# Quantiser extremes of seven matrices taken in the first projections instead of in the opening

## The chip, the cores and the metric

One core of one Trainium2 chip. The time is that of the whole program on the device in microseconds, the median of several runs. Beside it stands one execution recorded by the hardware profiler; all durations of single instructions come from it.

## What is computed

Two transformer blocks on x, 4096 rows of 256 (4 batches of 1024). The first one, L0, has 16 heads of 16 and quantises each weight matrix as a whole to 8 bits before use; the second, L1, has 16 heads of 64 and plain weights.

```python
def fake_quant_w(w, n_bits=NBITS):
    levels = 2 ** n_bits - 1
    mn = jnp.min(w)
    mx = jnp.max(w)
    delta = (mx - mn) / levels
    zp = jnp.round(-mn / delta)
    wq = jnp.clip(jnp.round(w / delta) + zp, 0, levels)
    wdq = (wq - zp) * delta
    return w + jax.lax.stop_gradient(wdq - w)
...
x = cross_attn(layernorm(x, ln1_g, ln1_b), layernorm(x, ln1_g, ln1_b), q1_w, k1_w, v1_w, o1_w, o1_b) + x
x = cross_attn(layernorm(x, ln2_g, ln2_b), context, q2_w, k2_w, v2_w, o2_w, o2_b) + x
x = geglu_ff(layernorm(x, ln3_g, ln3_b), ff1_w, ff1_b, ff2_w, ff2_b) + x
```

So ten matrices of L0 need a minimum and a maximum over all their elements, and a division, before any of their elements can be quantised: `q1_w`, `k1_w`, `v1_w` and the seven that the kernel calls LATE: `o1_w`, `k2_w`, `v2_w`, `q2_w`, `o2_w`, `ff1_w`, `ff2_w`.

## The kernel before

The program is a row of phases. Each opens its buffers and semaphores, gives every engine one written-out list of instructions, and ends with all engines done and its semaphores cleared. Every engine (SP is a queue of DMA issues) goes through its list in order; a `wait_ge` holds all that stands behind it on that engine.

1. `quantise`. SP loads all ten matrices, then x. VectorE (DVE) takes maximum and negated minimum of each (L288, L289), PE transposes the column of extremes and spreads the result over the partitions (L274, L276), DVE works out five scalars per matrix (`self.scalars`: delta, its reciprocal, zero point, two halves of -delta), then quantises the three matrices that are needed at once in ten turns, and SP stores them.
2. `norm_project` of L0. Eight tiles of 512 rows. In a tile: layer norm (DVE statistics, GpSimd `norm_rstd`, DVE `norm_xhat`, PE transposes, ACT scale), a split of the rows into a high and a low part (ACT `high_rows`, DVE `low_rows`), and four chunks c = 0 to 3 of q and k and four units of v on PE, each as six matmuls of high and low parts. DVE and ACT evict them, SP stores them. The norm of tile t + 2 and `low_rows(t + 1)` (L747, at c == 3) are put between the evictions of tile t. PE waits at the start of each tile for `hi_done` and `lo_done`.
3. `attend_narrow`, the self attention of L0. 16 steps i of 16 slots s. In a slot DVE takes four row maxima of scores for a later step (`top`, L1369), PE makes scores (L1501) and shifted scores (L1518), ACT exponentiates them (L1481), PE multiplies with the values (L1530). Four banks hold what DVE reads, three what ACT reads. The same lists hold the once-only work. DVE: `negate`, `turned`, `normalise`, `low`, `project`. SP: `load(i + 2)`, then `maxima(i + 1)`, and at i == 0 the load of the quantised `o1_w` into `wraw` (L1339), once it is stored. GpSimd: memsets, the addition of the bias to x, then `late_quantise`, which quantises the seven late matrices in 11 pieces of at most 1024 columns (five of 512 columns, six of 1024), 14 instructions each, with the loads and stores issued by GpSimd itself (L396, L428). Ahead of piece 4 it splits `wraw` (`low_weights`, L1350).
4. Cross attention and feed forward of L0, then the same phases of L1 with their own weights.

ACT splits `wraw` too; where it does so is this (L1466 to L1469):

```python
for i in range(STEPS + 1):
    if i == 1:
        act.wait_ge(w_in, 16)
        a_.activation(w_hi[:, :, :], wraw[:, :, :], ACT.Copy).then_inc(w_high, 1)
    for s in range(SLOTS if i < STEPS else 10):
```

`w_hi` is first needed in `project` of step 3, within step 4.

Of the kernel before, what the change touches and what calls it, by code (L numbers as in the profile page):

```python
# [96 lines left out]
class Program:  # L97
# [113 lines left out]
    def quantise(self, x_sb, ident):  # L211
# [4 lines left out]
        for name, rows in mats:  # L216
# [3 lines left out]
            self.wq[name] = nc.dram_tensor("quantised_" + name, (i, o), F32, kind="Internal").ap()  # L220
        K = len(mats)
        now = range(K - len(self.LATE))
        size = where[K - len(self.LATE)][0]
        with ExitStack() as st:
            sb, ps, sem = self.open(st)
            w, t, rest = sb("w", [P, at]), sb("t", [P, size]), sb("rest", [P, size])
# [4 lines left out]
            delta, rdelta, zp, ndh, ndl = (self.scalars[:, k, :] for k in range(5))  # L231
# [4 lines left out]
            w_in = [sem("w_in_" + name) for name, _ in mats]  # L236
            ext_t, ends_b = sem("ext_t"), sem("ends_b")
# [126 lines left out]

    LATE_SIZE = 1024

    def late_buffers(self, sb, sem):
# [6 lines left out]
    def late_quantise(self, pool, s, at_piece, between):  # L374
        g = self.nc.gpsimd
        pieces = []
        for m, name in enumerate(self.LATE):
            i, o = self.i["L0_xattn_" + name].shape
            p = 96 if name in ("k2_w", "v2_w") else P
            rows = min(i, max(1, self.LATE_SIZE // o) * p)  # L380
            for a in range(0, i, rows):
                for b in range(0, o, self.LATE_SIZE):
                    cols = slice(b, min(b + self.LATE_SIZE, o))
                    pieces.append((m, *(x[a:a + rows, cols].rearrange("(c p) n -> p c n", p=p)
                                        for x in (self.i["L0_xattn_" + name], self.wq[name]))))

        shapes = [(src.shape[0], src.shape[1] * src.shape[2]) for _, src, _ in pieces]

# [3 lines left out]
        def load(n):  # L392
            m, src, _ = pieces[n]
            if n >= 2:
                pool.wait_ge(s["out"][n % 2], 16 * (n // 2))
# [33 lines left out]
        for k in range(2):  # L429
            pool.wait_ge(s["out"][k], 16 * ((len(pieces) + 1 - k) // 2))  # L430

# [217 lines left out]

    def norm_project(self, L, x_sb, ident, g, b, wq, wk, wv):  # L650
        nc = self.nc
        planes = (self.q, self.k)
        per = L.dim // P
# [20 lines left out]
        with ExitStack() as st:  # L674
# [11 lines left out]
            c_out = [sem(f"c_out{k}") for k in range(ring)]  # L686
            v_out = [sem(f"v_out{k}") for k in range(2)]
            block = st.enter_context(nc.Block())
# [52 lines left out]
            def _(dve):  # L741
                v = nc.vector

                def low_rows(t):
# [9 lines left out]
                self.norm_xhat(dve, n, x_sb, 1)  # L754
                for t in range(TILES):
# [467 lines left out]
    def attend_narrow(self, L, x_sb, ident, wo, bo):  # L1223
# [43 lines left out]
        with ExitStack() as st:  # L1267
# [32 lines left out]
            def _(sp):  # L1300
# [29 lines left out]
                for i in range(STEPS):  # L1330
# [28 lines left out]
            def _(dve):  # L1359
# [2016 lines left out]
    def build(self):  # L3376
        nc, i = self.nc, self.i
        with ExitStack() as st:
# [3 lines left out]
            self.kept = [st.enter_context(nc.semaphore(f"pool_stored{k}")) for k in range(2 * 3 * 2)]  # L3382
            self.scalars = st.enter_context(nc.sbuf_tensor("quantise_scalars", [P, 5, 10], F32))
            self.late_sems = [st.enter_context(nc.semaphore(f"late_{x}{k}")) for x in ("in", "out") for k in range(2)]
            self.quantise(x_sb, ident)

            def p(name):
                return i["L0_xattn_" + name]
# [5 lines left out]
            L, L1 = Layer("L0", 16, 4, None), Layer("L1", 64, 2, None)  # L3394
            self.norm_project(L, x_sb, ident, p("ln1_g"), p("ln1_b"), q["q1_w"], q["k1_w"], q["v1_w"])
            self.attend_narrow(L, x_sb, ident, q["o1_w"], p("o1_b"))
# [32 lines left out]
```

## Time and profile before

| | |
|---|---|
| median of 3 runs | 4222.43 us (4221.16 to 4227.47) |
| profiled execution | 4226.14 us, span 4224.3 us |
| granted TensorE clock, mean over the span | 0.948 |
| busy share of the span | PE 93%, DVE 65%, ACT 44%, POOL 44% |

How to read it: PE is the matmul engine, DVE VectorE, ACT ScalarE, POOL GpSimd, SP the queue that issues most transfers. A line such as L1369 is one of the kernel file. Times of a timeline count from the start of the span. `[0.53 <-ACT f_h_hi L778]` says that the engine was idle for 0.53 us ahead of the instruction and what released it. The granted clock (PEclk) is a share of 2.4 GHz, so 0.50 is 1.2 GHz. A busy PE is not a PE at its peak.

### The profile page before, as it was taken

How to read it: one execution, taken by the hardware profiler on the slowest of the kernel's cores; microseconds unless marked ns; L12 is line 12 of the kernel's file. 1: busy time of each engine (PE TensorE's matmuls, PEld its weight loads, DVE VectorE, ACT ScalarE, POOL GpSimd, SP SyncE). 2: the span in 40 equal slices, each digit the busy share in tenths (PEclk: the TensorE clock that was granted, in tenths of full speed). 3: DMA queues.
4: the chain of work that ended last, by engine and by line, in shares of the span. 5: the costliest groups of instructions: out<-in, count | busy, mean ns of one | idle time of the engine just before them, and what ended most of it. 6: DMA issues, size and time to landing. Idle time of an engine off the chain costs nothing. (4 is left out here: it accounts for less than half of the span.)

```text
span 4224.3 us, 64439 instructions
## 1 busy us (share of the span) xinstructions
PE 3916.2 (93%) x24639; PEld 2597.8 (61%) x24639; DVE 2766.8 (65%) x4547; ACT 1839.8 (44%) x2746; POOL 1859.1 (44%) x1203
## 2 busy tenths in 40 slices
PE   3799999995898997998999999999999979999899
PEld 2543443433456886885666666666666647777787
DVE  6599999953446654435767666676767637665665
ACT  1367777771453333442333333333333324444333
POOL 1288970001113102004777877877787753222200
PEclk9789999986779998997999999999999989999999
DMA  4734434405631105883211121111112010000100
GB/s 158 181 56 75 60 57 46 45 1 79 106 54 49 25 13 177 305 308 123 73 54 51 51 76 51 51 57 70 51 51 73 29 31 10 10 10 1 42 14 17
DMA packets 314325, 294.96 MB, mean 70 GB/s; under 512 B 133324, under 2 KB 237196, under 8 KB 313764
## 3 DMA queue, kind: packets, MB, share of 16 engines
q1 hardware_dynamic: 311364, 281.88, 25.8%
q0 software_dynamic: 2656, 8.97, 0.7%
q8 instruction: 197, 3.23, 0.3%
q14 instruction: 108, 0.88, 0.1%
HBM read 161.92 MB, written 127.28 MB: 68 GB/s over the span
## 5 line engine op out<-in xcount | busy, mean ns | idle before, releaser
L1741 POOL TENSOR_TENSOR f_sums<-f_sums,f_probs 128x1024 f32<-128x1024 f32 x384 | 915.5, 2384 | 154.6 <-ACT f_probs L1860 116.9
L1860 ACT ACTIVATE f_probs<-f_st 128x1024 f32<-128x1024 f32 x512 | 525.0, 1027 | 938.6 <-PE f_st L1906 933.9
L1758 DVE TENSOR_REDUCE f_mx<-f_s 128x1 f32<-128x512 f32 x1024 | 659.8, 686 | 381.0 <-PE f_s L1883 369.6
L1369 DVE TENSOR_REDUCE f_mx<-f_s 128x1 f32<-128x512 f32 x1024 | 638.7, 683 | 53.2 <-PE f_s L1501 31.2
L1481 ACT ACTIVATE f_probs<-f_st 128x512 f32<-128x512 f32 x1024 | 536.1, 600 | 234.1 <-PE f_st L1518 233.8
L1883 PE MATMUL f_s<-f_k,f_q 64*128 64x512 f32 x3072 | 514.7, 414 | 19.1 <-DMA f_k<-k 12.9
L1906 PE MATMUL f_st<-f_q,f_k 64*128 64x512 f32 x3072 | 486.0, 390 | 1.1 <-ACT f_probs L1860 1.0
L1920 PE MATMUL f_acc<-f_probs,f_v 128*64 128x512 f32 x2048 | 466.1, 597 | 0.0
L1883 PEld LDWEIGHTS f_s<-f_k,f_q 64*128 64x128 f32 x3072 | 341.4, 189 | 166.8 <-issue 112.5
L1906 PEld LDWEIGHTS f_st<-f_q,f_k 64*128 64x128 f32 x3072 | 367.0, 185 | 25.8 <-ACT f_probs L1860 3.8
L1518 PE MATMUL f_st<-f_q,f_k 50*128 50x512 f32 x1024 | 336.1, 480 | 6.6 <-ACT f_probs L1481 6.4
L588 POOL TENSOR_TENSOR f_ve<-f_var,f_const 128x4 f32<-128x4 f32 x48 | 10.0, 209 | 698.4 <-DVE f_var L569 698.2
L1518 PEld LDWEIGHTS f_st<-f_q,f_k 50*128 50x128 f32 x1024 | 137.5, 188 | 283.7 <-ACT f_probs L1481 262.6
L1920 PEld LDWEIGHTS f_acc<-f_probs,f_v 128*64 128x64 f32 x2048 | 141.5, 137 | 266.1 <-issue 257.2
L1501 PE MATMUL f_s<-f_k,f_q 48*128 48x512 f32 x1024 | 267.9, 457 | 22.8 <-DMA f_k<-k 22.5
L1530 PE MATMUL f_acc<-f_probs,f_v 128*32 128x512 f32 x2048 | 279.3, 619 | 0.0
L1781 DVE RECIPROCAL f_rd<-f_s 128x512 f32<-128x512 f32 x64 | 214.9, 3358 | 71.7 <-PE f_s L1929 71.7
L1906 PE MATMUL f_st<-f_m,f_mones 64*128 64x512 f32 x1024 | 248.4, 390 | 0.0
L3281 ACT ACTIVATE f_gate<-f_pg,f_bias 128x512 f32<-128x512 f32 x128 | 88.0, 688 | 348.8 <-PE f_pg L3327 348.8
L765 DVE TENSOR_TENSOR f_stage<-f_pc,f_stage 128x512 f32<-128x512 f32 x160 | 110.3, 691 | 190.2 <-ACT f_stage L795 190.1
L1737 POOL TENSOR_TENSOR f_sums<-f_probs 128x1024 f32<-128x1024 f32 x64 | 153.2, 2394 | 184.0 <-ACT f_probs L1860 184.0
L3206 DVE SCALAR_TENSOR_TENSOR f_u<-f_pa,f_bias,f_gate 128x512 f32<-128x512 f32 x128 | 96.1, 751 | 201.4 <-PE f_pa L3327 195.7
(320 smaller groups left out, 7861.8 us busy)
## 6 DMA issues: line engine op xcount, KB each, us to landing
q<-f_stage SPq DMA_DIRECT2D x80, 512.0 KB, 2.9
k<-f_stage SPq DMA_DIRECT2D x80, 512.0 KB, 2.8
f_q<-q SPq DMA_DIRECT2D x32, 1024.0 KB, 5.1
f_k<-k SPq DMA_DIRECT2D x32, 1024.0 KB, 7.5
v<-f_v_stage SPq DMA_DIRECT2D x64, 256.0 KB, 3.1
f_v<-v SPq DMA_DIRECT2D x32, 512.0 KB, 8.7
f_q<-q SPq DMA_DIRECT2D x96, 128.0 KB, 4.3
f_k<-k SPq DMA_DIRECT2D x96, 128.0 KB, 7.1
```

The source lines that it names most:

```text
L1369: v.tensor_reduce(mx[:, i % 2, c:c + 1], bank[u % 4][:, :], AX_X, ALU.max).then_inc(s_free, 1)
L1481: a_.activation(probs[:, n % NP, e % 2, :], stb[k % 3][:, :], ACT.Exp, scale=L.scale).then_inc(p_ready, 1)
L1501: t.matmul(bank[u % 4][:, :], q[cur][rows, j, qb * P:(qb + 1) * P], k_[cur][rows, j, f * HALF:(f + 1) * HALF], start=True, stop=True, tile ...
L1518: t.matmul(stb[n % 3][:, :], k_[cur][rows, j, c * P:(c + 1) * P], q[cur][rows, j, half * HALF:(half + 1) * HALF], start=True, stop=True, t ...
L1530: ins = t.matmul(acc[W * h:W * h + W, :], vs[cur][:, c, h, :], p, start=c == 0, stop=c == KC - 1, tile_position=(0, W * h))
L1741: g_.tensor_tensor(out, out, probs[:, n % NP, :, :], ALU.add).then_inc(sum_done, 1)
L1758: v.tensor_reduce(mx[:, i % 2, c:c + 1], bank[u % 3][:, :], AX_X, ALU.max).then_inc(s_free, 1)
L1781: v.reciprocal(rd[:, half, :], bank[u % 3][:, :]).then_inc(s_free, 1)
L1860: a_.activation(probs[:, s % NP, :, :], stb[s % 2][:, :, :], ACT.Exp, scale=L.scale).then_inc(p_ready, 1)
L1883: ins = t.matmul(bank[u % 3][:, :], q[cur][rows, a, qb * P:(qb + 1) * P], k_[cur][rows, c, f * HALF:(f + 1) * HALF], start=r == 0, stop=r ...
L1906: ins = t.matmul(stb[s % 2][:, h, :], lhs, rhs, start=r == 0, stop=r == 3, tile_position=(64 * h, 0))
L1920: ins = t.matmul(acc[W * h:W * h + W, :], vs[cur][:, c, h, :], probs[:, s % NP, h, :], start=c == 0, stop=c == KC - 1, tile_position=(0, W ...
```

## The change

The opening loads and reduces three matrices in place of ten, and its scalar chain works on three columns in place of ten. The extremes of the seven others are taken piece by piece (the same 11 pieces) in `norm_project` of L0: SP loads the pieces behind the weights, DVE reduces one at c == 1 and one at c == 3 of each tile from tile 2 on. Their 128 x 2 x 11 row extremes are written to DRAM by GpSimd in `attend_narrow` and read back to all partitions; DVE reduces them at i == 0, s == 12 (`late_ends`); GpSimd works out the scalars from them in 40 chained instructions (`late_scalars`) and then quantises the pieces as before. The load of `wraw` waits for 32 in place of 16 on the semaphore that now also counts the write of the row extremes.

```diff
-                for j, (name, rows) in enumerate(mats):
+                for j, (name, rows) in enumerate(mats[0:K]):
                     sp.dma_start(chunks(w, j), dram_view(ins["L0_xattn_" + name], j)).then_inc(w_in[j], 16)
...
+    def late_ends(self, dve, s):
+        v = self.nc.vector
+        dve.wait_ge(s["out"][1], 16)
+        counts = [sum(1 for p in self.late_pieces() if p[0] == m) for m in range(len(self.LATE))]
+        singles = counts.count(1)
+        assert counts[:singles] == [1] * singles
+        for x, op, out in ((0, ALU.max, s["span"]), (1, ALU.min, s["low"])):
+            v.tensor_reduce(out[:, 0:singles], s["rows"][:, x, 0:singles, :], AX_X, op).then_inc(s["top"], 1)
+            at = singles
+            for m in range(singles, len(counts)):
+                v.tensor_reduce(out[:, m:m + 1], s["rows"][:, x, at:at + counts[m], :].rearrange("p k n -> p (k n)"), AX_X, op)\
+                    .then_inc(s["top"], 1)
+                at += counts[m]
+
+    def late_scalars(self, pool, s, c):
...
+        g.dma_start(self.late_rows.rearrange("(x k p) -> p x k", p=P, x=2), self.late_ext[:, :, :], allow_slow_non_contiguous=True)\
+            .then_inc(s["out"][0], 16)
+        pool.wait_ge(s["out"][0], 16)
+        g.dma_start(s["rows"][:, :, :, :].rearrange("p x k m -> p (x k m)"), self.late_rows.partition_broadcast(P))\
+            .then_inc(s["out"][1], 16)
+        c.done(g.memset(levels, float(LEVELS)))
+        c.done(g.memset(rlevels, 1.0 / LEVELS))
+        chained(g.memset(minus, -1.0))
+        pool.wait_ge(s["out"][1], 16)
+        pool.wait_ge(s["top"], 2 * 3)
+        chained(g.tensor_tensor(low, low, minus, ALU.mult))
+        chained(g.tensor_tensor(span, span, low, ALU.add))
...
+        chained(g.tensor_tensor(rdelta, delta, minus, ALU.pow))
...
+        chained(g.tensor_scalar(zp, left, MAGIC, -MAGIC, ALU.add, ALU.add))
...
+        c = Count(pool, s["step"])
         load(0)
-        c = Count(pool, s["step"])
+        self.late_scalars(pool, s, c)
         for k, (m, src, dst) in enumerate(pieces):
...
+                for k, (_, src, _) in enumerate(late):
+                    sp.dma_start(late_w[k][0:src.shape[0], :].rearrange("p (c n) -> p c n", c=src.shape[1]), src).then_inc(late_in[k], 16)
                 for t in range(TILES):
...
+                def extreme(k):
+                    src = late[k][1]
+                    piece_k = late_w[k][0:src.shape[0], :]
+                    dve.wait_ge(late_in[k], 16)
+                    dve.wait_ge(late_done, 2)
+                    for x, op in ((0, ALU.max), (1, ALU.min)):
+                        v.tensor_reduce(self.late_ext[0:src.shape[0], x, k:k + 1], piece_k, AX_X, op).then_inc(late_done, 1)
...
                 for t in range(TILES):
                     for c in range(chunks):
+                        k = ((t - LATE_TILE) * chunks + c) // 2
+                        if c % 2 == 1 and 0 <= k < len(late):
+                            extreme(k)
                         if c == 0 and t + 2 < TILES:
...
                     if i == 0:
-                        sp.wait_ge(late["out"][0], 16)
+                        sp.wait_ge(late["out"][0], 32)
                         sp.dma_start(wraw[:, :, :], wo.rearrange("(c p) d -> p c d", p=P)).then_inc(w_in, 16)
...
                             if f == 0 and s == 10 and i < STEPS:
                                 normalise(2 * i)
+                            if f == 0 and s == 12 and i == 0:
+                                self.late_ends(dve, late)
```

## Rows read from the trace of the kernel before

**Rows 1.** The page, costliest groups: busy us, mean ns; idle before, releaser.

```profile
L1369 DVE TENSOR_REDUCE f_mx<-f_s 128x1 f32<-128x512 f32 x1024 | 638.7, 683 | 53.2 <-PE f_s L1501 31.2
```

**Rows 2.** Timeline of the opening: start us, busy us, engine, line, operation.

```profile
8.27 0.69 DVE L288 TENSOR_REDUCE f_ext<-f_w 128x1 f32<-128x512 f32 x1
...
24.95 2.28 DVE L288 TENSOR_REDUCE f_ext<-f_w 128x1 f32<-128x2048 f32 x1
...
29.57 0.37 PE L274 MATMUL f_pt<-ident,f_ext 128*20 128x128 f32 x1 [29.57 <-DVE f_ext L289]
```

**Rows 3.** Timeline of DVE in one tile of the first projections.

```profile
105.17 0.69 DVE L765 TENSOR_TENSOR f_stage<-f_pc,f_stage 128x512 f32<-128x512 f32 x1 [2.06 <-ACT f_stage L795]
...
107.49 0.69 DVE L765 TENSOR_TENSOR f_stage<-f_pc,f_stage 128x512 f32<-128x512 f32 x1 [0.34 <-ACT f_stage L795]
108.71 1.22 DVE L747 TENSOR_TENSOR f_h_lo<-f_ht,f_h_hi 128x1024 fp32r<-128x1024 f32 x1 [0.53 <-ACT f_h_hi L778]
```

**Rows 4.** Timeline of PE at the edge between two tiles.

```profile
109.14 0.28 PE L827 MATMUL f_pv<-f_w_hi,f_h_lo 128*128 128x256 f32 x1
110.04 0.47 PE L817 MATMUL f_pc<-f_h_hi,f_w_hi 128*128 128x512 f32 x1 [0.62 <-issue]
```

**Rows 5.** Windows: stretch, length, PE, PEld, DVE, ACT, POOL busy, PEclk, DMA, GB/s.

```profile
0.00:56.00 56.00, 0.98 (x3) 0.59 (x3) 44.17 (x81) 0.00 (x0) 0.70 (x6) 1.00 0.56 180
56.00:78.00 22.00, 6.72 (x23) 5.17 (x24) 10.89 (x38) 6.05 (x8) 8.81 (x20) 0.97 0.13 36
```

**Rows 6.** Timeline of GpSimd, small chained instructions of the layer norm.

```profile
59.00 1.02 POOL L590 TENSOR_TENSOR f_rstd<-f_ve,f_const 128x4 f32<-128x4 f32 x1
60.10 0.20 POOL L592 TENSOR_TENSOR f_tmp<-f_rstd 128x4 f32<-128x4 f32 x1
60.38 0.20 POOL L594 TENSOR_TENSOR f_tmp<-f_tmp,f_ve 128x4 f32<-128x4 f32 x1
```

**Rows 7.** Timeline of GpSimd, and one row of DVE, in the self attention.

```profile
220.56 0.95 POOL L396 DMA_DIRECT2D f_late_w<-L_xattn_o_w  x1
...
223.90 0.69 POOL L414 TENSOR_SCALAR f_late_t<-f_late_w,quantise_scalars 128x512 f32<-128x512 f32 x1 [1.69 <-DMA f_late_w<-L_xattn_o_w]
...
246.09 0.82 POOL L428 DMA_DIRECT2D quantised_o_w<-f_late_w  x1 [0.30 <-POOL f_late_w L427]
249.01 0.65 POOL L396 DMA_DIRECT2D f_late_w<-L_xattn_v_w  x1 [2.10 <-DMA quantised_o_w<-f_late_w]
...
329.31 1.29 POOL L1350 TENSOR_TENSOR f_w_lo<-f_wraw,f_w_hi 128x512 fp32r<-128x512 f32 x1
...
429.09 0.69 DVE L1415 TENSOR_TENSOR x_rows<-x_rows,f_s 128x512 f32<-128x512 f32 x1 [0.40 <-PE f_s L1560]
```

**Rows 8.** DMA issues of the whole run: count, KB each, median us to landing.

```profile
f_v<-v SPq DMA_DIRECT2D x128, 32.0 KB, 6.1
...
f_late_w<-L_xattn_ff_w POOLq DMA_DIRECT2D x6, 512.0 KB, 4.1
```

**Rows 9.** Timeline of the self attention around the end of step 0.

```profile
264.50 2.48 DVE L1369 TENSOR_REDUCE f_mx<-f_s 128x1 f32<-128x512 f32 x4
...
271.48 0.58 SPq L1339 DMA_DIRECT2D f_wraw<-quantised_o_w  x1
...
274.61 0.65 ACT L1469 ACTIVATE f_w_hi<-f_wraw 128x512 fp32r<-128x512 f32 x1
```

**Rows 10.** Windows of the granted clock, columns as in rows 5.

```profile
162.00:228.00 66.00, 43.99 (x79) 20.99 (x80) 44.71 (x77) 0.00 (x0) 31.40 (x16) 0.50 0.64 75
...
242.00:246.00 4.00, 4.00 (x23) 2.02 (x23) 2.81 (x5) 2.73 (x6) 3.63 (x3) 0.78 0.01 4
```

**Rows 11.** Timeline of the slots of step 0, PE and ACT.

```profile
235.82 1.93 PE L1530 MATMUL f_acc<-f_probs,f_v 128*32 128x512 f32 x8
...
239.88 1.93 PE L1530 MATMUL f_acc<-f_probs,f_v 128*32 128x512 f32 x8
...
272.68 2.06 ACT L1481 ACTIVATE f_probs<-f_st 128x512 f32<-128x512 f32 x4 [0.54 <-PE f_st L1518]
```

More of the change, by code:

```diff
@@ L220, in quantise @@
             self.wq[name] = nc.dram_tensor("quantised_" + name, (i, o), F32, kind="Internal").ap()
-        K = len(mats)
-        now = range(K - len(self.LATE))
-        size = where[K - len(self.LATE)][0]
+        K = len(mats) - len(self.LATE)
+        now = range(K)
+        size = where[K][0]
+        self.late_rows = nc.dram_tensor("late_extremes", (2 * self.LATE_PIECES * P,), F32, kind="Internal").ap()
         with ExitStack() as st:
             sb, ps, sem = self.open(st)
-            w, t, rest = sb("w", [P, at]), sb("t", [P, size]), sb("rest", [P, size])
+            w, t, rest = sb("w", [P, size]), sb("t", [P, size]), sb("rest", [P, size])
             ext = sb("ext", [P, 2 * K])
@@ L230, in quantise @@
             ends = sb("ends", [P, 2 * K])
-            delta, rdelta, zp, ndh, ndl = (self.scalars[:, k, :] for k in range(5))
+            delta, rdelta, zp, ndh, ndl = (self.scalars[:, k, 0:K] for k in range(5))
             span, levels, rlevels = sb("span", [P, K]), sb("levels", [P, K]), sb("rlevels", [P, K])
@@ L235, in quantise @@
             x_in, id_done, v_done, stored = sem("x_in"), sem("id"), sem("v"), sem("st")
-            w_in = [sem("w_in_" + name) for name, _ in mats]
+            w_in = [sem("w_in_" + name) for name, _ in mats[0:K]]
             ext_t, ends_b = sem("ext_t"), sem("ends_b")
@@ L365 @@
     LATE_SIZE = 1024
+    LATE_PIECES = 11
     def late_buffers(self, sb, sem):
@@ L371, in late_buffers, with late_pieces @@
         s["step"] = sem("late_step")
-        return s
-    def late_quantise(self, pool, s, at_piece, between):
-        g = self.nc.gpsimd
+        n, m = self.LATE_PIECES, len(self.LATE)
+        s["rows"], s["top"] = sb("late_rows", [P, 2, n, P]), sem("late_top")
+        for k in ("span", "low", "levels", "rlevels", "minus", "high_q", "low_q", "left", "part"):
+            s[k] = sb("late_" + k, [P, m])
+        return s
+    def late_pieces(self):
         pieces = []
@@ L385, in late_quantise @@
                                         for x in (self.i["L0_xattn_" + name], self.wq[name]))))
+        assert len(pieces) == self.LATE_PIECES
+        return pieces
+    def late_ends(self, dve, s):
[11 more added lines that the diff above has]
+                at += counts[m]
@@ new lines, in late_scalars, with chained, split, less @@
+    def late_scalars(self, pool, s, c):
+        g = self.nc.gpsimd
+        K = len(self.LATE)
+        first = self.scalars.shape[2] - K
+        delta, rdelta, zp, ndh, ndl = (self.scalars[:, k, first:] for k in range(5))
+        span, low, levels, rlevels, minus, h, l, left, part = (s[k][:, :] for k in (
+            "span", "low", "levels", "rlevels", "minus", "high_q", "low_q", "left", "part"))
+        def chained(ins):
+            c.done(ins)
+            c.wait()
+        g.dma_start(self.late_rows.rearrange("(x k p) -> p x k", p=P, x=2), self.late_ext[:, :, :], allow_slow_non_contiguous=True)\
[10 more added lines that the diff above has]
+        chained(g.tensor_tensor(span, span, low, ALU.add))
+        def split(num):
+            chained(g.tensor_scalar(ndh, num, float(4097), None, ALU.mult))
+            chained(g.tensor_tensor(left, ndh, num, ALU.subtract))
+            chained(g.tensor_tensor(ndh, left, ndh, ALU.subtract))
+            chained(g.tensor_tensor(ndl, num, ndh, ALU.add))
+            chained(g.tensor_tensor(ndl, ndl, minus, ALU.mult))
+        def less(q, d):
+            chained(g.tensor_tensor(part, q, d, ALU.mult))
+            chained(g.tensor_tensor(left, left, part, ALU.add))
+        split(levels)
+        chained(g.tensor_tensor(delta, span, rlevels, ALU.mult))
+        chained(g.tensor_scalar(h, delta, float(4097), None, ALU.mult))
+        chained(g.tensor_tensor(l, h, delta, ALU.subtract))
+        chained(g.tensor_tensor(h, h, l, ALU.subtract))
+        chained(g.tensor_tensor(l, delta, h, ALU.subtract))
+        chained(g.tensor_tensor(part, h, ndh, ALU.mult))
+        chained(g.tensor_tensor(left, span, part, ALU.add))
+        less(l, ndh)
+        less(h, ndl)
+        less(l, ndl)
+        chained(g.tensor_tensor(left, left, rlevels, ALU.mult))
+        chained(g.tensor_tensor(delta, delta, left, ALU.add))
+        chained(g.tensor_tensor(rdelta, delta, minus, ALU.pow))
+        chained(g.tensor_tensor(part, rdelta, delta, ALU.mult))
+        chained(g.tensor_scalar(part, part, -1.0, 2.0, ALU.mult, ALU.add))
+        chained(g.tensor_tensor(rdelta, rdelta, part, ALU.mult))
+        split(delta)
+        chained(g.tensor_tensor(h, low, rdelta, ALU.mult))
+        chained(g.tensor_scalar(h, h, MAGIC, -MAGIC, ALU.add, ALU.add))
+        chained(g.tensor_tensor(left, h, ndh, ALU.mult))
+        chained(g.tensor_tensor(left, left, low, ALU.add))
+        less(h, ndl)
+        chained(g.tensor_tensor(left, left, rdelta, ALU.mult))
+        chained(g.tensor_tensor(left, left, h, ALU.add))
+        chained(g.tensor_scalar(zp, left, MAGIC, -MAGIC, ALU.add, ALU.add))
@@ L387, in late_quantise @@
+    def late_quantise(self, pool, s, at_piece, between):
+        g = self.nc.gpsimd
+        pieces = self.late_pieces()
         shapes = [(src.shape[0], src.shape[1] * src.shape[2]) for _, src, _ in pieces]
@@ L394, in load @@
             if n >= 2:
-                pool.wait_ge(s["out"][n % 2], 16 * (n // 2))
+                pool.wait_ge(s["out"][n % 2], 16 * (n // 2 + 1))
             g.dma_start(part(s["w"][n % 2], n).rearrange("p (c n) -> p c n", c=src.shape[1]), src).then_inc(s["in"][n % 2], 16)
+        c = Count(pool, s["step"])
         load(0)
-        c = Count(pool, s["step"])
+        self.late_scalars(pool, s, c)
         for k, (m, src, dst) in enumerate(pieces):
@@ L429, in late_quantise @@
         for k in range(2):
-            pool.wait_ge(s["out"][k], 16 * ((len(pieces) + 1 - k) // 2))
+            pool.wait_ge(s["out"][k], 16 * ((len(pieces) + 1 - k) // 2 + 1))
     def context_kv(self, L, wk, wv):
@@ L647, with norm_project @@
     H_PASSES = [(k, a, b) for k in range(DC) for a, b in ((0, 0), (0, 1), (1, 0))]
-    def norm_project(self, L, x_sb, ident, g, b, wq, wk, wv):
+    def norm_project(self, L, x_sb, ident, g, b, wq, wk, wv, extremes=False):
         nc = self.nc
+        late = self.late_pieces() if extremes else []
+        LATE_TILE = 2
         planes = (self.q, self.k)
@@ L687, in norm_project @@
             v_out = [sem(f"v_out{k}") for k in range(2)]
+            if extremes:
+                late_w = [sb(f"late_w{k}", [P, src.shape[1] * src.shape[2]]) for k, (_, src, _) in enumerate(late)]
+                late_in, late_done = [sem(f"late_in{k}") for k in range(len(late))], sem("late_done")
             block = st.enter_context(nc.Block())
@@ L754, in _ @@
                 self.norm_xhat(dve, n, x_sb, 1)
+                if extremes:
+                    v.memset(self.late_ext[:, 0, :], -3.0e38).then_inc(late_done, 1)
+                    v.memset(self.late_ext[:, 1, :], 3.0e38).then_inc(late_done, 1)
                 for t in range(TILES):
                     for c in range(chunks):
+                        k = ((t - LATE_TILE) * chunks + c) // 2
+                        if c % 2 == 1 and 0 <= k < len(late):
+                            extreme(k)
                         if c == 0 and t + 2 < TILES:
@@ L3383, in build @@
             self.scalars = st.enter_context(nc.sbuf_tensor("quantise_scalars", [P, 5, 10], F32))
+            self.late_ext = st.enter_context(nc.sbuf_tensor("late_ext", [P, 2, self.LATE_PIECES], F32))
             self.late_sems = [st.enter_context(nc.semaphore(f"late_{x}{k}")) for x in ("in", "out") for k in range(2)]
@@ L3394, in build @@
             L, L1 = Layer("L0", 16, 4, None), Layer("L1", 64, 2, None)
-            self.norm_project(L, x_sb, ident, p("ln1_g"), p("ln1_b"), q["q1_w"], q["k1_w"], q["v1_w"])
+            self.norm_project(L, x_sb, ident, p("ln1_g"), p("ln1_b"), q["q1_w"], q["k1_w"], q["v1_w"], extremes=True)
             self.attend_narrow(L, x_sb, ident, q["o1_w"], p("o1_b"))
```

## The prediction, written before the change was run

> **What bounds the kernel now.** I read the page first, then the timeline of the opening, of one tile of the first projections and of the first two steps of the self attention, with the windows for the granted clock and DMA. The opening is one chain on DVE: the reductions of ten matrices, then a scalar chain and the ten turns of three matrices. PE makes no step before the last extreme: its transpose waits until 29.57, while the first late reduction starts at 8.27 [rows 2]. In the projections PE sets the pace, but each tile starts with a wait: the last matmul of a tile is issued at 109.14, the next tile's first at 110.04 [rows 4], just after `low_rows` ends at 108.71 + 1.23 = 109.94 [rows 3]. In the self attention DVE's 1024 maxima (638.7 us busy, 53.2 us idle in all) set the pace [rows 1], one slot of four per 2.6 us, and ACT has only some 0.5 us of room per slot [rows 11]. PE, DVE and ACT each go through a written-out order, tied by a few PSUM banks: a wait of some ten us on one is a wait of all three.
>
> **The opening.** The fourteen late reductions go: 29.57 - 8.27 is 21.3 us, less 0.1 for the end of the reduction before, so **-21.2 us**. The scalar chain that follows has as many instructions as before, 10 columns or 3 wide, and costs the same. The load of x still lands in time: before it stood behind 4.3 MB more. The seven late loads move to the projections, as 11 issues on SP behind three weight loads.
>
> **Their transfer** runs in a stretch where DMA is busy 0.13, in before's time 60 to 78. 4.3 MB at the 180 GB/s of the opening's average take 24 us, up to 84 [rows 5]. The first tile's stores begin only as this stretch ends, and SP has nothing else to issue before them, so its 11 issues hold up nobody. I take 0 and keep +4 for the range, for what of the transfer reaches past 78. If this cover went, the first tile's stores would be late, then ACT's stage, then PE.
>
> **DVE in the projections.** A 512-wide reduction takes 0.69 us, four in a row 2.48, so 0.60 each [rows 2, 9]; 2048 wide take 2.28 [rows 2], so 1.04 ns per column, and 1024 wide 1.13 us in a row. A pair (maximum and minimum) costs 1.2 us for pieces 0 to 4 and 2.27 for 5 to 10. Pieces with even number stand at c = 1, in an idle 2.06 us [rows 3]: nothing, or 0.2. Odd ones stand before `low_rows`, where idle time is only 0.53 [rows 3], and this is the instruction that PE waits for at the tile's edge [rows 4]. Pieces 1 and 3 cost 0.67 each, 5, 7 and 9 cost 1.74 each: **+6.6 us**. Bounds: 0 if PE's own work hid it, +12 if the whole 20 us of DVE work less its idle time at c = 1 came through.
>
> **The self attention.** This part decides. Before, GpSimd quantises `o1_w` from 223.90, its store is issued at 246.09 and has landed by 249.01 [rows 7]; SP loads it after its maxima at 271.48, and ACT splits it at 274.61 with no idle time before it [rows 9]. That ACT instruction stands at i == 1 ahead of all exponentials of step 1, behind `act.wait_ge(w_in, 16)`, and the change leaves it there. Now the piece can't start before its scalars, and these wait for `late_ends`, which DVE does at i == 0, s == 12. In before's time:
> - Two of the four maxima that start at 264.50 are done at 265.7; `late_ends` starts there [rows 9]. It reads 640, 512 and 256 columns, twice each: 2 x (0.73 + 0.60 + 0.34) = 3.3 us, done at 269.0.
> - GpSimd then issues 40 chained instructions. A small chained one takes 0.28 from start to start (60.10 to 60.38), a power 1.10 (59.00 to 60.10) [rows 6]; 39 x 0.28 + 1.1 = 12.0. The row's power is 4 wide and this one 7, so I take 12.5: 281.5. Bounds 12 to 18: no small tensor_scalar of GpSimd is in the trace.
> - The issue of load(1), 0.7; then piece 0 to landing, 249.01 - 223.90 = 25.1 [rows 7]: 307.3.
> - SP's issue to ACT's split, 274.61 - 271.48 = 3.1 [rows 9]: 310.4.
>
> ACT stood there at 274.61, so step 1 starts **35.8 us** later. What queues behind it: ACT's exponentials; PE's `shifted`, after three banks; PE's scores behind that; DVE's maxima behind those; SP's load(3), which waits for `pv_done`. The 3.3 us of `late_ends` are within the 35.8 and not added. PE runs ahead by under a slot and gets nothing back, since its own time per slot is nearly full.
>
> **The clock.** In the first 66 us around the start of the self attention PE was idle for 22; the granted clock fell to 0.50 (1.2 GHz) and was back only in 242 to 246, at 0.78 on average [rows 10]. At the low level a slot takes 239.88 - 235.82 = 4.06 us, at 2.4 GHz 2.06 + 0.54 = 2.60 [rows 11], so 1.46 us a slot. With its values matmuls PE came back some 7 us after 235.82: two slots, **+3 us**. Bounds 0 and the rival below.
>
> **Of no cost.** The sum moves GpSimd's pieces by 58 us: the split of `wraw` at 329.31 goes to about 388, its first use stands just before 429.09 [rows 7], itself 36 later. The two transfers of the row extremes start at about 221.5, behind load(0) [rows 7], and DVE asks for them at 265.7, 44 us later. The first writes 2816 single elements. 512 short runs land in 6.1 us [rows 8]; one after the other 2816 take 34 us, overlapped far less. The second fills 128 partitions with 1.4 MB; 512 KB land in 4.1 [rows 8], so 11.5. 34 + 11.5 + 2 for the issues is 47, 3 us late at the worst; I take about 20 and no wait. By the Trainium skill (DMA: Bandwidth & Descriptors, Anatomy of one DMA) a transfer from GpSimd costs about 2 us plus bytes over 436 GB/s, which would make the second 5.3 us, an estimate that the 4.1 us for 512 KB agrees with only roughly (3.2 by the rule). Its Rules for kernel authors say that a strided last dimension becomes one descriptor per element, which speaks against the first; no row here shows a store of single elements.
>
> **Sum:** -21.2 + 6.6 + 35.8 + 3 = **+24.2 us**. The profiled execution took 4226.14 us (span 4224.3), 3.7 above the median of the runs, 4222.43; against the first it gives 4250.3, against the median, which is what is timed, 4246.6: **4247 us**.
>
> **Rivals.** What a measurement of this kernel can tell from no change is about 0.2%, 8.4 us.
> - *The stall, as summed* (0.76): 4234 to 4260 (the projections at 0 or 12, the clock at 0 or 8, the chain at 12 or 18, not all at once).
> - *The clock stays low long* (0.05). From 182 to 242 PE was at work and the clock stayed at 0.50: 44 us of busy time before 228 [rows 10], some 58 in all. If it took as long again, 58 / 4.06 = 14 slots x 1.46 = 21 us in place of 3: 4265. Against it: in 182 to 228 PE did nearly only scores of 48 rows. The Trainium skill (TensorE: Matmul & The Clock Gate, What's actually happening) says that the low clock is the default and that activity releases it; by that rule the trace agrees that idling costs, and 4265 hangs on how much PE's mix counts.
> - *DVE waits for the row extremes* (0.07). Its place is `late_ends`; it decides from a landing later than 265.7 on, one for one. With both transfers at 60 us in all it adds 16: 4263.
> - *The other side: ACT isn't held* (0.05). What speaks for it: before, ACT had no idle time at its split [rows 9]. The opening's gain then stands against 6.6 and the 3.3 of `late_ends`: -11.3, 4211. It needs `late_ends` done by 233 instead of 269, against DVE's order; so it would take an order of instructions other than I read.
> - *The two sides nearly cancel* (0.07): the stall at under 30 us, with free extremes and no clock cost. GpSimd would do its 37.6 us of chain and piece in 30 while DVE stands still: 4222.43 - 21.2 + 29 = 4230.
>
> Faster 0.05, same 0.07, slower 0.88. The range reaches from 4232 to 4263: it takes in the first case nearly whole and the wait of DVE, and leaves out the low clock's end, the cancelling and the faster case, 17 in 100 together, and a little of the first case's edges.
>
> **What the profile after would show.** The transpose on PE at about 8.4; `norm_project` starting at about 35; a gap at each tile's edge from tile 2 on, 0.7 then 1.7 us longer. In step 0 of the self attention six reductions at s == 12 without idle time before them; GpSimd's 40 small instructions in about 12.5 us; then an idle time of ACT before its split of some 32 to 36 us, released by the load of `wraw`, with PE and DVE idle as long, and some slots at 1.2 GHz after it. The prediction is wrong if ACT has no such idle time, if GpSimd's chain is far from 12 us, or if DVE sits ahead of `late_ends` waiting for the broadcast.

## The result, and the profile after

The changed kernel takes 4249.75 us (median of 3 runs, 4248.9 to 4258.63) against 4222.43: ratio 1.0073, 95% interval 1.0058 to 1.0089, so it is slower. The ratio isn't the quotient of the two medians: they differ by 27.3 us, the ratio stands for 30.8. The profiled execution of it took 4258.63 us (span 4256.8, mean granted clock 0.945); it was the longest of its three, and is 32.5 us over the profiled one of before. The comparison by place below uses starts of the same instruction in both traces.

The opening, on PE and DVE (timeline; columns as in [rows 2]). The transpose starts at 7.97, in [rows 2] at 29.57:

```profile
7.15 0.68 DVE L290 TENSOR_REDUCE f_ext<-f_w 128x1 f32<-128x512 f32 x1
7.97 0.37 PE L275 MATMUL f_pt<-ident,f_ext 128*6 128x128 f32 x1 [7.97 <-DVE f_ext L290]
```

One tile edge of the first projections, DVE and then PE (timeline). It answers to [rows 3, 4]:

```profile
107.41 0.69 DVE L874 TENSOR_TENSOR f_stage<-f_pc,f_stage 128x512 f32<-128x512 f32 x1 [0.34 <-ACT f_stage L904]
108.01 2.34 DVE L851 TENSOR_REDUCE late_ext<-f_late_w 128x1 f32<-128x1024 f32 x2
110.27 1.22 DVE L842 TENSOR_TENSOR f_h_lo<-f_ht,f_h_hi 128x1024 fp32r<-128x1024 f32 x1
...
111.58 0.47 PE L926 MATMUL f_pc<-f_h_hi,f_w_hi 128*128 128x512 f32 x1 [2.25 <-issue]
...
114.33 1.91 PE L706 MATMUL f_tp<-ident,f_xhat 128*128 128x128 f32 x8
```

`low_rows` (L842) now starts right behind the pair (L851), with no idle time, and PE's gap at the edge is 2.25 us instead of 0.62. The windows that follow show what the gap costs besides itself (columns as in [rows 5]; the clock is the third value from the end):

```profile
110.00:112.00 2.00, 0.41 (x2) 0.40 (x3) 2.00 (x4) 0.00 (x0) 0.00 (x0) 1.00 0.52 145
112.00:114.00 2.00, 2.00 (x11) 1.78 (x10) 1.93 (x10) 0.60 (x1) 0.00 (x0) 0.77 0.51 182
114.00:116.00 2.00, 2.00 (x12) 2.00 (x11) 1.97 (x5) 0.38 (x1) 1.48 (x4) 0.50 0.66 199
```

The clock falls from 1.00 to 0.50 some 1.5 us after PE resumed (0.77 is its mean over 112 to 114). `low_rows` starts at 77.03, 87.76, 98.48, 110.27, 123.64 and 135.43: 0.57, 0.56, 1.63, 3.21 and 1.63 more than the 10.16 us of before, and the last tile loses 1.5 too. The 3.21 holds 1.58 of the low clock.

GpSimd and then DVE at the start of the self attention (timelines); the forecast has nothing that answers to it:

```profile
204.62 1.41 POOL L420 DMA_DIRECT2D late_extremes<-late_ext  x1
220.96 0.57 POOL L423 DMA_DIRECT2D f_late_rows<-late_extremes  x1 [14.94 <-DMA late_extremes<-late_ext]
```

```profile
208.02 7.26 DVE L1478 TENSOR_REDUCE f_mx<-f_s 128x1 f32<-128x512 f32 x12
222.71 3.68 DVE L1478 TENSOR_REDUCE f_mx<-f_s 128x1 f32<-128x512 f32 x6 [7.43 <-PE f_s L1612]
```

DMA issues in the same stretch, 200 to 225 (count, KB each, median us to landing):

```profile
f_late_rows<-late_extremes POOLq DMA_DIRECT2D x1, 1408.0 KB, 11.1
...
f_q<-f_mm SPq DMA_DIRECT2D x4, 8.0 KB, 11.3
late_extremes<-late_ext POOLq DMA_DIRECT2D x1, 11.0 KB, 16.1
```

and of before, in its stretch 214 to 240:

```profile
f_q<-f_mm SPq DMA_DIRECT2D x4, 8.0 KB, 1.9
```

The store of the row extremes took 16.1 us to land. The transfers that put the row maxima into `f_q`, issued after it, landed in 11.3 us instead of 1.9, and PE's next scores, and so DVE, waited 7.4 us for them. The first row maximum of the phase is 14.4 us earlier than before (168.19 against 182.60), the first exponential only 6.0 (222.28 against 228.25).

The end of step 0, all engines (timeline), to be set beside [rows 7, 9]:

```profile
257.13 0.81 DVE L401 TENSOR_REDUCE f_late_span<-f_late_rows 128x5 f32<-128x640 f32 x1
257.86 1.00 DVE L404 TENSOR_REDUCE f_late_span<-f_late_rows 128x1 f32<-128x512 f32 x2
...
260.69 0.20 POOL L430 TENSOR_TENSOR f_late_low<-f_late_low,f_late_minus 128x7 f32<-128x7 f32 x1 [38.97 <-DVE f_late_low L404]
260.97 0.20 POOL L431 TENSOR_TENSOR f_late_span<-f_late_span,f_late_low 128x7 f32<-128x7 f32 x1
...
267.01 1.52 POOL L457 TENSOR_TENSOR quantise_scalars<-quantise_scalars,f_late_minus 128x7 f32<-128x7 f32 x1
...
273.88 0.80 POOL L483 DMA_DIRECT2D f_late_w<-L_xattn_k_w  x1 [0.30 <-POOL quantise_scalars L469]
...
296.86 0.81 POOL L516 DMA_DIRECT2D quantised_o_w<-f_late_w  x1 [0.30 <-POOL f_late_w L515]
...
299.50 0.38 SPq L1448 DMA_DIRECT2D f_wraw<-quantised_o_w  x1
...
302.30 0.63 ACT L1580 ACTIVATE f_w_hi<-f_wraw 128x512 fp32r<-128x512 f32 x1 [31.65 <-DMA f_wraw<-quantised_o_w]
...
307.31 3.74 DVE L1478 TENSOR_REDUCE f_mx<-f_s 128x1 f32<-128x512 f32 x6 [33.40 <-PE f_s L1612]
```

This is the forecast chain: extremes, 40 small instructions, one piece, its store, SP's load, ACT's split. ACT stands idle for 31.65 us and is 27.7 later than in [rows 9]; DVE behind it stands for 33.4. What idle time DVE has before its row maxima, 53.2 us in [rows 1], is now 91.6:

```profile
L1478 DVE TENSOR_REDUCE f_mx<-f_s 128x1 f32<-128x512 f32 x1024 | 638.5, 682 | 91.6 <-PE f_s L1612 69.5
```

From here the distance stays: the phases that follow start 31.4, 28.6, 30.8, 30.2, 30.0 and 30.5 us later than before.

### The profile page after: what moved, and what is told of

Its sections match the earlier page's. It is cut to its first block and busy times, and to the rows that moved or that the text cites. A ratio compares the mean times of both kernels' runs of the same rounds, so it can differ in the third digit from the quotient of the medians.

```text
span 4256.8 us, 64515 instructions
## 1 busy us (share of the span) xinstructions
PE 3924.2 (92%) x24639; PEld 2604.0 (61%) x24639; DVE 2773.1 (65%) x4563; ACT 1837.9 (43%) x2746; POOL 1869.2 (44%) x1248
## 3 DMA queue, kind: packets, MB, share of 16 engines
q0 software_dynamic: 2864, 10.42, 0.9%
## 5 line engine op out<-in xcount | busy, mean ns | idle before, releaser
L1478 DVE TENSOR_REDUCE f_mx<-f_s 128x1 f32<-128x512 f32 x1024 | 638.5, 682 | 91.6 <-PE f_s L1612 69.5
```

Of the source, the lines that this page charges most:

```text
L1478: v.tensor_reduce(mx[:, i % 2, c:c + 1], bank[u % 4][:, :], AX_X, ALU.max).then_inc(s_free, 1)
```

## The experiments

An edit is shown against the changed kernel, and a ratio is to the kernel before, run on the same chip. Single executions of the kernel before lay between 4208.6 and 4241.4 us there, wider than its first three, so the ratios carry the comparison. The changed kernel stands at 1.0073, from its own three executions; it wasn't run again beside the experiments. 0.001 is 4.2 us. An interval reaches some 6 to 9 us to either side, and the difference of two ratios is uncertain by some 9 to 11 us, so single us are read from the traces.

**ACT's split at step 3**

```diff
-                    if i == 1:
+                    if i == 3:
                         act.wait_ge(w_in, 16)
```

> One edit on the changed kernel: ACT splits wraw at i == 3 in place of i == 1. Theory A (the stall is ACT's wait for wraw ahead of the exponentials of step 1): the 31.7 us idle time of ACT is gone, its 27.7 us of shift and the 1.3 us after it too, and 3.3 us of late_ends show instead; SP still waits at i == 0 for the store of o1_w until about 300, so load(3) and maxima(2) are late and cost 4 to 6 us. Time 4218 to 4223, against 4215 without SP's part. Rival B (another engine would be held as long by the late quantised weights, PE at w_low or SP's queue): most of the stall comes back elsewhere, time over 4235.

Measured: 4236.07 us, ratio 1.0031 (1.0016 to 1.0046). ACT passes the end of step 0 without a wait for `wraw`, and 18 us of the 31 over before are gone. That is 13 us above the 4218 to 4223 expected: SP's part was priced at 4 to 6 us. The rest is the same wait on SP, whose load of `wraw` stands ahead of `load(3)`. SP and ACT of this kernel (timeline):

```profile
301.44 0.38 SPq L1448 DMA_DIRECT2D f_wraw<-quantised_o_w  x1
301.86 2.80 SPq L1418 DMA_DIRECT2D f_q<-q  x6
...
319.94 1.08 ACT L1592 ACTIVATE f_probs<-f_st 128x512 f32<-128x512 f32 x2 [6.78 <-PE f_st L1629]
322.92 1.08 ACT L1592 ACTIVATE f_probs<-f_st 128x512 f32<-128x512 f32 x2 [1.90 <-PE f_st L1629]
```

`load(3)` is issued at 301.86; with SP free (next kernel) at 278.16. Its data are missing at 313 to 320, and some slots at 1.2 GHz follow. Step 2's output is evicted 11.6 us later than before in the trace: a queue behind the same instruction holds the engines a second time.

**ACT's split at step 3 and SP's load at step 2**

```diff
-                    if i == 0:
+                    if i == 2:
                         sp.wait_ge(late["out"][0], 32)
                         sp.dma_start(wraw[:, :, :], wo.rearrange("(c p) d -> p c d", p=P)).then_inc(w_in, 16)
```

> As the run before, and SP loads wraw at i == 2 in place of i == 0, so nothing in SP's list waits for GpSimd in steps 0 and 1. Theory A: 4215, some 5 us under the run with ACT's edit alone, and load(3) issued as soon as step 1 has begun. If SP's wait cost nothing, both give the same time.

Measured: 4222.76 us, ratio 0.999 (0.9975 to 1.0005). 35 us less than the changed kernel (1.0073 - 0.999), and 8 more than the 4215 expected: without the wait for the first quantised matrix, on the two engines that ask for it early, the whole loss is gone. What is left is no clear gain, though the opening is 21.6 us shorter: the delays of the projections and of the first step's scores are still in it. Another reason stands in the trace at `late_ends`:

```profile
260.95 1.01 DVE L404 TENSOR_REDUCE f_late_low<-f_late_rows 128x1 f32<-128x512 f32 x2
...
268.32 2.48 DVE L1478 TENSOR_REDUCE f_mx<-f_s 128x1 f32<-128x512 f32 x4 [2.03 <-PE f_s L1612]
```

with the windows of this kernel:

```profile
260.00:264.00 4.00, 0.54 (x2) 0.32 (x2) 3.96 (x9) 0.83 (x2) 1.37 (x7) 0.79 0.00 0
264.00:268.00 4.00, 4.00 (x16) 1.58 (x18) 2.26 (x6) 1.19 (x3) 2.89 (x15) 0.50 0.03 6
```

PE is busy for 0.54 of 4 us while DVE does its six reductions, and then runs at 0.50.

**`late_ends` at s == 4**

```diff
-                            if f == 0 and s == 12 and i == 0:
+                            if f == 0 and s == 4 and i == 0:
                                 self.late_ends(dve, late)
```

> One edit on the changed kernel: late_ends at slot 4 of step 0 in place of slot 12, ACT's wait left where it is. Theory A: the sum from late_ends to ACT's split (41.8 us) stays, and starts 8 slots of 2.6 us earlier: 21 us less, 4229, ACT idle about 11 us. The broadcast landed at 232 and slot 4 comes at about 236, so DVE should not wait. Rival B (GpSimd's work decides by its own length, wherever late_ends stands, or DVE waits for the broadcast): less than 10 us gained.

Measured: 4239.32 us, ratio 1.0035 (1.0019 to 1.005), 16 us less than the changed kernel. ACT's split, in this kernel's timeline:

```profile
287.16 0.63 ACT L1580 ACTIVATE f_w_hi<-f_wraw 128x512 fp32r<-128x512 f32 x1 [8.00 <-DMA f_wraw<-quantised_o_w]
```

`late_ends` starts at 241.73, 15.4 us earlier; the split 15.1 earlier. One for one: the chain from DVE's extremes to ACT's split sets the time. It isn't the 21 us expected, because step 0 itself begins later in this trace: the first exponential is at 227.28 instead of 222.28, behind a wait of DVE of 10.24 us. ACT's idle time shrinks by more, 31.65 to 8.00, because ACT's last exponentials before the split end 8.5 us later: 5.0 are that later beginning, the rest the slots at 1.2 GHz that follow `late_ends` (three ACT waits of 2.99, 1.89 and 1.70).

**Row extremes stored as 128 rows of 88 bytes**

```diff
-        g.dma_start(self.late_rows.rearrange("(x k p) -> p x k", p=P, x=2), self.late_ext[:, :, :], allow_slow_non_contiguous=True)\
+        g.dma_start(self.late_rows.rearrange("(p x k) -> p x k", p=P, x=2), self.late_ext[:, :, :])\
```

and `late_ends` reads with a stride of 88 bytes instead.

> The 2816 row extremes are stored as 128 rows of 88 bytes in place of 2816 single elements, and late_ends reads the broadcast with a stride. Theory C (the store of single elements, 16.1 us to landing, holds back the small transfer of row maxima by some 9 us, and PE waits for it at the start of step 0): the transfer of the maxima lands in some 2 us, first exponentials 8 us earlier, and since the clock comes back later in exchange, 5 to 8 us less: 4242 to 4245. Rival D (it is the traffic of load(2), or the 1.4 MB broadcast, that holds the maxima back): no change beyond 2 us. A strided reduction on DVE may cost up to some us more; the rows of late_ends will show it.

Measured: 4253.94 us, ratio 1.0065 (1.0047 to 1.0084): in the total not told apart from the changed kernel. The trace shows both halves. DMA issues, 203 to 228, and DVE:

```profile
f_q<-f_mm SPq DMA_DIRECT2D x4, 8.0 KB, 6.7
late_extremes<-late_ext POOLq DMA_DIRECT2D x1, 11.0 KB, 2.7
```

```profile
219.61 7.40 DVE L1478 TENSOR_REDUCE f_mx<-f_s 128x1 f32<-128x512 f32 x12 [2.69 <-PE f_s L1612]
...
253.87 1.61 DVE L401 TENSOR_REDUCE f_late_span<-f_late_rows 128x5 f32<-128x640 f32 x1
```

The store lands in 2.7 us instead of 16.1, DVE waits 2.69 instead of 7.43, and the first exponential is 3.1 earlier. But the strided reads make `late_ends` 5.0 us instead of 3.3, and the row maxima are still at 6.7 us, not 1.9. The load that follows the store (1.4 MB) now falls into the same time, but that it is the cause isn't shown: in the second and fourth of the versions below, with the same rows, the maxima land in 1.9 and 3.7 us, and DVE waits 3.02 and 3.05 us all the same. So the singles cost 3 to 6 us here, not the 8 that the trace of the changed kernel seems to show.

**The pair of extremes behind `low_rows`**

```diff
-                        if c % 2 == 1 and 0 <= k < len(late):
-                            extreme(k)
...
                         if c == LOW_AT and t + 1 < TILES:
                             low_rows(t + 1)
+                        if c % 2 == 1 and 0 <= k < len(late):
+                            extreme(k)
```

> The changed kernel with one edit: in the first projections the pair of extremes is reduced after low_rows of the same chunk, not ahead of it. Theory (the pair delays low_rows, and the longer gap of PE at the tile's edge lets its clock dip): low_rows starts 10.2 us apart in tiles 2 to 7 again in place of 10.7 to 13.4, the granted clock stays 1.00 through the projections, the next phase starts some 9 us earlier than in the changed kernel, and the whole is 6 to 9 us less than its 4249.75: 4241 to 4244. Rival (DVE is nearly full in these tiles, so the reductions only delay the evictions instead, and the stages they hold up): 0 to 3 us less, 4247 to 4250. The stall of ACT in the self attention stays as long (31 to 32 us idle) in both.

Measured: 4250.35 us, ratio 1.0072 (1.0052 to 1.0092), no gain; the theory fell. `low_rows` waits for no pair now, but starts 10.16, 11.67, 11.71, 12.51 and 11.59 us apart, in the end nearly as late as in the changed kernel (134.63 and 135.43), and the clock again falls at two edges, behind gaps of PE of 2.13 and 2.98 us. In the tile of 11.67 us (timeline, DVE, SP, ACT and PE):

```profile
88.29 1.27 DVE L851 TENSOR_REDUCE late_ext<-f_late_w 96x1 f32<-96x512 f32 x2
...
92.81 1.27 DVE L851 TENSOR_REDUCE late_ext<-f_late_w 96x1 f32<-96x512 f32 x2
...
92.92 0.36 SPq L805 DMA_DIRECT2D q<-f_stage  x1
93.32 1.31 SPq L811 DMA_DIRECT2D v<-f_v_stage  x1
...
95.36 0.38 ACT L908 ACTIVATE f_v_stage<-f_pv 128x256 f32<-128x256 f32 x1 [1.62 <-DMA v<-f_v_stage]
...
100.14 0.71 PE L926 MATMUL f_pc<-f_h_hi,f_w_hi 128*128 128x512 f32 x1 [2.13 <-issue]
```

The pair now delays the evictions of DVE; SP issues its stores in order and stands behind them, the stores of v among them; ACT waits 1.62 us for its v buffer, `high_rows` comes late, and PE's gap at the edge is back (2.13). So the delay moved to another engine. Is DVE too full in these tiles, or does any delayed eviction harm? Before, DVE was busy 7.12 of 10.16 us in a tile; two pairs of 1024 columns add 4.67, which is more than fits, one adds 2.34. But the two pairs of 512 columns of this tile add only 2.54, which fits, and it still took 11.67 us. What is full there is a part of the tile: DVE has no idle time from `low_rows` at 87.15 to the eviction that ends at 94.67, since the pair of c == 3 and the next tile's pair of c == 1 stand close together.

**One pair per tile, and five in the gaps of the first two tiles**

```diff
                 low_rows(0)
+                    for k in range(4):
+                        extreme(k)
                 self.norm_xhat(dve, n, x_sb, 1)
...
-                        if c % 2 == 1 and 0 <= k < len(late):
-                            extreme(k)
...
+                        if extremes and t == 1 and c == 0:
+                            extreme(4)
+                        if extremes and 1 <= t <= 6 and c == 1:
+                            extreme(4 + t)
```

> The changed kernel with the eleven pairs of extremes at other places of DVE's list in the first projections: the four of 512 columns that come first stand ahead of norm_xhat(1), where DVE was idle 5.0 us; piece 4 behind the statistics at t == 1, c == 0, idle 2.9 us; pieces 5 to 10 one per tile at c == 1 of tiles 1 to 6, none at c == 3. Theory (in tiles 3 to 6 two pairs of 2.3 us are more than the 2.9 us that DVE is idle in a tile of 10.2, so DVE sets the pace there whichever of them stands first; one pair per tile fits): the tiles are 10.2 to 10.5 us apart, the next phase starts 6 to 9 us earlier than in the changed kernel (152.1), at 143 to 146, and the total is 6 to 9 us less: 4241 to 4244, ratio to the kernel before 1.005. Rival (any delay of an eviction at c == 1 delays the stores of SP and with them ACT's staging buffers): tiles 11 us or more apart, 0 to 3 us less in all.

Measured: 4249.88 us, ratio 1.0053 (1.0032 to 1.0073). In the trace the projections are as forecast (DVE, timeline, and a window):

```profile
107.74 1.22 DVE L842 TENSOR_TENSOR f_h_lo<-f_ht,f_h_hi 128x1024 fp32r<-128x1024 f32 x1 [0.54 <-ACT f_h_hi L890]
112.21 2.34 DVE L851 TENSOR_REDUCE late_ext<-f_late_w 128x1 f32<-128x1024 f32 x2
117.90 1.23 DVE L842 TENSOR_TENSOR f_h_lo<-f_ht,f_h_hi 128x1024 fp32r<-128x1024 f32 x1 [0.54 <-ACT f_h_hi L890]
...
106.00:116.00 10.00, 9.38 (x57) 8.10 (x57) 9.12 (x21) 5.84 (x11) 2.20 (x7) 1.00 0.82 260
```

Tiles are 10.16 us apart again with 2.34 us of extremes in each, `low_rows` has its 0.54 of idle time back, the clock stays at 1.00, and the next phase opens at 143.10 instead of 152.11. So an eviction delayed by 2.34 us at c == 1 does no harm, since DVE catches up within the tile, and the rival falls. Against the run before two things differ: less work per tile, and no pair at c == 3. In the tiles of 512 columns the work alone can't be it (2.54 us there, 2.34 here); whether it is the place c == 3 or the two pairs so close together, no run separates. Of the 9.0 us the self attention gives back most, in this trace: ACT's split is at 299.02, only 3.3 earlier. The store of single elements again holds the scores, DVE for 9.68 us this time. By the ratios the total is 8 us less than the changed kernel, with an uncertainty of about 11.

**All together, in four versions**

The first has the two edits of the weights, the pair behind `low_rows`, and rows of 88 bytes:

> The changed kernel with four edits together: ACT splits the weights at step 3 and SP loads them at step 2, the pair of extremes stands after low_rows, and the row extremes are stored as 128 rows of 88 bytes (late_ends reads with a stride then). Theory (the costs add, since they sit at four places): from the 4222.8 of the two weight edits alone, 6 to 9 less for the projections and 1 to 3 less for the store: 4211 to 4216, ratio to the kernel before 0.996 to 0.998, and no idle time of ACT over 8 us in steps 0 to 3. Rival (what is gained before the self attention is lost again there to a longer time at the low clock): 4219 to 4223, with more slots of 4.06 us than in the changed kernel.

Measured: 4212.62 us, ratio 0.9984 (0.997 to 0.9999). The second puts the six reductions of `late_ends` one by one into slots 5 to 15:

> The same four edits, and the six reductions of late_ends are put one by one into slots 5, 7, 9, 11, 13 and 15 of step 0 instead of all at slot 12. Theory (six in a row, 5 us, leave PE idle long enough for its clock to fall again, which costs some 3 us more): no slot at the low clock after step 0's middle, and 2 to 4 us less than with all six at one place. Rival (DVE sets the pace, so 5 us of its work cost 5 us wherever they stand, and the clock doesn't matter here): within 1 us of it.

Measured: 4211.5 us, ratio 0.9982 (0.9968 to 0.9997), not told apart from the first in the total. In the traces the waits are. ACT with six reductions in a row:

```profile
258.73 1.09 ACT L1592 ACTIVATE f_probs<-f_st 128x512 f32<-128x512 f32 x2 [5.93 <-PE f_st L1629]
261.58 2.11 ACT L1592 ACTIVATE f_probs<-f_st 128x512 f32<-128x512 f32 x4 [1.77 <-PE f_st L1629]
```

and none over 1.2 us from 230 to 420 when they are spread. The third is the second with single elements again:

> As the version with the reductions spread over the slots, but the row extremes are stored as 2816 single elements again, so that late_ends reads contiguous rows (3.3 us in all, not 5.2). Theory (the store of single elements slows the row maxima of step 0 and PE waits for them): the first exponential some 3 us later than with the rows of 88 bytes, and the total 0 to 3 us more, since 1.9 us of DVE come back. Rival (the store costs nothing that lasts): the total 2 us less than with the rows.

Measured: 4217.61 us, ratio 0.9988 (0.9971 to 1.0005), too wide to settle the total. The trace does: the first exponential at 222.92 against 216.60, and DVE idle for 8.57 us in place of 3.02, with the first row maximum only 0.8 later. The store of single elements costs some 5.5 us at this place. The fourth has the weights' two edits, the extremes in the gaps, rows of 88 bytes and `late_ends` spread:

> That placement together with the weights split at step 3 and loaded at step 2, the row extremes stored as 128 rows of 88 bytes, and the six reductions of late_ends one per slot. Theory (each edit takes away a cost at its own place): 4 to 6 us less than the version that had the pair behind low_rows in place of this placement (4211.5): 4205 to 4208, ratio to the kernel before 0.996 to 0.9975. Rival (what the projections gain is waited for again at the load of q and k at the start of the self attention): the first row maxima start no earlier than 166.9, and the total stays at 4211.

Measured: **4207.81 us**, ratio 0.9962 (0.9946 to 0.9977), faster than both kernels: 16 us less than before. Here the earlier end of the projections lasts: GpSimd's first instruction of the self attention is at 141.67, and DVE's first row maximum at 159.64, 7.3 us before that of the second version. Spreading the six reductions doesn't keep the clock up in this trace, though: it is at 0.60 and 0.54 in 250 to 258, with an ACT wait of 1.89 us.

## Why the prediction was right, point by point

- **The opening**, -21.2: measured -21.6, some 0.5 of it a load that landed earlier. Right.
- **The transfer of the pieces**, 0: no pair waited for its piece, and the tiles before the first pair start 21.5 us earlier, as the opening does. Right.
- **DVE in the projections**, +6.6: measured +9.2 at their end. The pairs took 1.27 and 2.34 us, and PE's gap grew by 0.55 and 1.63 (forecast 0.67 and 1.74), so the term itself is 6.0. Mis-sized was the term of the clock: the prediction had it only in the self attention, yet gaps of 2.25 us brought two falls to 1.2 GHz here, 1.6 and 1.5 us. In the changed kernel the gap grows as forecast, by the pair's length less an idle time. But a second wait, through DVE's evictions and SP's stores, stood right behind it: moving the pair off `low_rows` gained nothing, one pair per tile at c == 1 gained all. (A slip without effect: the end of `low_rows` is 108.71 + 1.22 = 109.93.)
- **The chain of the self attention**, +35.8. From the start of `late_ends` to ACT's split: forecast 310.4 - 265.7 = 44.7, measured 302.30 - 257.13 = 45.2. In it `late_ends` 3.3 (3.3), the small instructions 12.9 (12.5), the power 1.52 for 7 columns, piece 0 with its landing 25.1 (25.1), SP to ACT 2.8 (3.1). Right to 0.5 us. ACT, PE and DVE stood as forecast. `late_ends` itself was to come at 265.7 - 21.2 + 6.6 = 251.1 and came at 257.13, 6.0 late: 2.2 of that are the two steps above, 5.8 the next one, and 2.0 came back, since the phase's first loads kept DVE waiting for 20.60 us and not 22.63.
- **Of no cost** is the step that failed. It asked whether DVE would wait for the row extremes, and rightly said no: they land near 232, DVE asks at 257. It did not ask whom the transfer itself would hold up. The store took 16.1 us (forecast about 20 for both transfers; 27 measured), the row maxima behind it 11.3 us instead of 1.9. Of the 14.4 us that the phase was ahead, 8.4 were gone at the first exponential. Some 2.6 came back: the clock returned after 10 us of step 0 here (0.68 in 230 to 234, 1.00 after), and after 16 before.
- **The clock behind the stall**, +3: 1.3 from the split to the next evictions. Two slots were forecast and about one was lost. The rival of a clock that stays low long fell: it was back at 308. The Trainium skill (TensorE: Matmul & The Clock Gate, What's actually happening) has activity release the low clock; by that rule the trace agrees here, where the clock came back within 6 us of the values matmuls. It doesn't agree at the start of the phase: in 182 to 228 of before PE was busy with scores of 48 rows for 43.8 of 46 us, and the clock stood at 0.50.
- **The sum**, +24.2: measured +27.3 in the medians, +30.8 by the ratio. At ACT's split the trace adds up: -21.6 for the opening, +9.2 for the projections, -2.0 for the first loads, +8.4 for the store, -2.6 for the clock that is back earlier, +36.3 from `late_ends` on (45.2 less the 8.9 from 265.7 to 274.61 of before): +27.7, and +29.0 with the clock behind the stall. Two misses of 2.6 and 5.8 us, and 0.5 in the chain, stand against gains of 2.0 and 0.4 and a clock that cost 1.3 and not 3. That the forecast came so near is in part this cancelling. That what comes ahead of `late_ends` counts one for one is shown by `late_ends` at s == 4.

The stall as the cause is shown from both sides: without it the loss is gone (0.999), and it is two waits: taking away ACT's gains 18 us, and then SP's 17 more, each uncertain by some 9. The prediction listed SP's `load(3)` only as queued behind ACT. In the changed kernel that holds, since SP has issued the load of `wraw` (299.50) before ACT goes on (302.30); but SP has a wait of its own, which shows once ACT's is gone.

## What to carry to other kernels

Work whose inputs now come later must have its readers moved too: look for each engine that waits for its output ahead of work that doesn't need it, and move the wait on all of them, or the second one takes the place of the first. When a small transfer is called free because its reader is late, ask also which transfers are issued behind it. And extra work on an engine that is not the bound is free only where that engine catches up before others wait for it: here one pair per tile at c == 1 cost nothing, and two per tile cost time in both places tried, because the wait only moved from PE's operand to SP's stores.

## What the runs showed of the hardware

- A store of 2816 single elements (11 KB) took 16.1 us to land, and the same bytes as 128 rows of 88 bytes 2.7 us. SP's transfers of 8 KB, issued 3 to 6 us after it, took 11.3 us, and 11.2 to 14.2 in the other traces with single elements, against 1.9 to 6.7 in those with rows. The Trainium skill (DMA: Bandwidth & Descriptors, Rules for kernel authors) has a strided last dimension lower to one descriptor per element; by that rule the trace agrees as far as the time goes, 5.7 ns an element. Its packets don't show 2816 of them: the software queue has 2864 in the whole run, and 2832 with rows of 88 bytes.
- TensorE's clock fell to 1.2 GHz after an idle time of 2.25 us between stretches of dense matmuls, at two of three such edges, after 2.13 and 2.98 us in the kernel with the pair behind `low_rows`, and behind the six reductions of `late_ends` in a row, where ACT waited 2.99 to 5.93 us. At 0.62 and 1.18 us it did not fall. Nor did it, in the trace of before, behind 4.00 us at 69.77 (1.00 in 70 to 76), while it was at 0.64 behind 3.48 us at 76.14.
- A maximum over 5 x 128 elements on DVE took 0.81 us contiguous and 1.61 with a stride of 88 bytes.
- Small chained GpSimd instructions take 0.28 us from start to start, 7 columns as well as 4, but the power 1.52 us with 7 and 1.02 with 4.
